# Routing of fourteen of sixteen token tiles moved into the attention stage ahead of it

## The reference

```python
scores = jnp.einsum('bsd,bmd->bsm', hidden_states, memory_tokens) * scale      # second attention
scores = jnp.where(memory_mask[:, None, :], scores, neg_inf)
attn = jax.nn.softmax(scores, axis=-1)
readout = jnp.einsum('bsm,bmd->bsd', attn, memory_tokens)
...
x = hidden_states.reshape(-1, hidden_shape[-1])                                # second mixture of experts
route = jax.nn.sigmoid(x @ router_w)
max_ind = jnp.argmax(route, axis=1)
max_prob = jnp.take_along_axis(route, max_ind[:, None], axis=1)
for e in range(num_experts):
    mask = (max_ind == e)[:, None]
    h = jax.nn.silu(x @ gate_w[e]) * (x @ up_w[e])
    out = out + jnp.where(mask, h @ down_w[e], 0.0)
out = out * max_prob
...
x = x + _L1_xattn_ref(_layernorm(x, axis=-1), ctx_2048, mask_BxS2_bk0)
x = x + _L1_ffn_ref(_layernorm(x, axis=-1), L1_ffn_router_w, L1_ffn_gate_w, L1_ffn_up_w, L1_ffn_down_w)
```

## Time and profile before

| | us |
|---|---|
| runs, median of 3 | 2923.95 (2922.61 to 2924.23) |
| the profiled execution | 2918.47, span 2916.6 |
| second attention, first work to last store issued | 2523.0 to 2715.7 |
| routing, first instruction to last | 2716.7 to 2761.5 |
| expert slots | from 2762.7 to the end |

### The profile page before, as it was taken

How to read it: one execution, slowest core, us unless ns; L and a number is a source line. 1 busy time by engine, 2 the same in 40 slices (tenths; PEclk the granted TensorE clock), 3 DMA queues, 4 the chain that set the end, 5 groups by cost and what they waited for, 6 DMA issues and landing times. The chain is left out here.

```text
span 2916.6 us, 57647 instructions
## 1 busy us (share of the span) xinstructions
PE 2780.5 (95%) x18157; PEld 2443.6 (84%) x18157; DVE 2052.8 (70%) x4824; ACT 1974.1 (68%) x4918; POOL 1697.1 (58%) x2124
## 2 busy tenths in 40 slices
PE   7989999799999999999999999999999997699698
PEld 5768888699999999999999999999999984499655
DVE  7974454577777777777777777777777758866444
ACT  5656666677777777777777777777777747666211
POOL 6766663365665665665666666556656537387122
PEclk9999999899999999999999999999999989899699
DMA  5447767612111111211111111121111014464510
GB/s 181 134 145 213 209 206 206 205 43 71 56 43 61 52 56 43 70 56 43 70 51 48 48 66 56 43 71 56 43 64 49 15 50 91 120 195 131 191 37 27
DMA packets 284601, 263.44 MB, mean 90 GB/s; under 512 B 46382, under 2 KB 260527, under 8 KB 284304
## 3 DMA queue, kind: packets, MB, share of 16 engines
q1 hardware_dynamic: 264784, 238.94, 25.8%
q10 hardware_dynamic: 17312, 15.73, 1.9%
q0 software_dynamic: 2208, 5.12, 0.6%
HBM read 167.34 MB, written 84.93 MB: 86 GB/s over the span
## 5 line engine op out<-in xcount | busy, mean ns | idle before, releaser
L1030 ACT ACTIVATE w_hi<-ps_t 128x512 fp32r<-128x512 f32 (+2 forms) x1024 | 568.4, 555 | 352.3 <-PE ps_t L1273 343.8
L1132 DVE TENSOR_TENSOR w_lo<-ps_t,w_hi 128x512 fp32r<-128x512 f32 (+2 forms) x1024 | 655.7, 640 | 178.8 <-ACT w_hi L1030 175.4
L1106 DVE TENSOR_REDUCE piece_max<-ps_s 128x1 f32<-128x512 f32 (+1 forms) x768 | 472.2, 622 | 238.2 <-PE ps_s L1260 221.6
L1293 PE MATMUL ps_o<-w_hi,v_hi 128*128 128x256 f32 (+1 forms) x1856 | 596.4, 321 | 0.0
L1203 POOL TENSOR_SCALAR prob<-prob,inv_sum 128x512 f32<-128x512 f32 (+2 forms) x768 | 477.8, 641 | 189.2 <-DVE inv_sum L1122 189.2
L1295 PE MATMUL ps_o<-w_hi,v_lo 128*128 128x256 f32 (+1 forms) x1856 | 523.6, 282 | 0.0
L1294 PE MATMUL ps_o<-w_lo,v_hi 128*128 128x256 f32 (+1 forms) x1856 | 522.3, 281 | 0.0
L1273 PE MATMUL ps_t<-ident,prob 128*128 128x128 f32 (+1 forms) x2784 | 517.8, 273 | 0.0
L1273 PEld LDWEIGHTS ps_t<-ident,prob 128*128 128x128 f32 (+1 forms) x2784 | 356.7, 140 | 62.8 <-DVE w_lo L1132 8.7
L1258 PE MATMUL ps_s<-k_hi,q_hi 128*128 128x512 f32 (+2 forms) x1024 | 395.9, 387 | 10.2 <-PEq L57 4.8
L1259 PE MATMUL ps_s<-k_lo,q_hi 128*128 128x512 f32 (+2 forms) x1024 | 377.6, 369 | 0.0
(11 more groups left out here) (288 smaller groups left out, 6352.3 us busy)
## 6 DMA issues: line engine op xcount, KB each, us to landing
v_scratch<-v_out SPq DMA_DIRECT2D x120, 256.0 KB, 3.0
raw_k<-k_scratch SPq DMA_DIRECT2D x32, 960.0 KB, 7.0
raw_v<-v_scratch SPq DMA_DIRECT2D x32, 960.0 KB, 4.7
k_scratch<-k_out SPq DMA_DIRECT2D x104, 256.0 KB, 2.7
q_scratch<-out_t SPq DMA_DIRECT2D x64, 256.0 KB, 2.5
r_all<-r_scratch SPq DMA_DIRECT2D x32, 512.0 KB, 4.2
raw_q<-q_scratch SPq DMA_DIRECT2D x32, 512.0 KB, 5.2
first_prob<-in_ctx_t ACTq DMA_DIRECT2D x50, 256.0 KB, 2.8
```

The source lines that it names most:

```text
L1030: nc.scalar.activation(pt_hi[keys, k % RING, cols], ps_t[keys, k % 2, cols], ACT.Copy).then_inc(hi_done, 1)
L1106: nc.vector.tensor_reduce(piece_max[:, n % 2, p:p + 1], ps_s[:, p, lo - p * PC:hi - p * PC], AX.X, ALU.max).then_inc(max_ready, 1)
L1132: nc.vector.tensor_tensor(pt_lo[keys, k % RING, cols], ps_t[keys, k % 2, cols], pt_hi[keys, k % RING, cols].bitcast(F32), ALU.subtract).th ...
L1293: nc.tensor.matmul(out, v_hi[gi][keys, vs], pt_hi[keys, k % RING, cols], start=blk == (0 if qt else 1), stop=False)
```

## The change

- The router, mean and variance, root, scores, best score and index become tensors that the attention fills for tiles 0 to 13 (`EARLY_ROUTED` is 14). `route_to_slots` does these steps for tiles 14 and 15 alone, and then goes on as before.
- In the attention, tile t is measured by DVE in unit t + 1 behind `add_x` (and behind the penalty where there is one). POOL takes its root at the end of unit t + 1. DVE normalises its rows in step 0 of unit t + 2, behind the inverse sum. PE turns the two halves of the rows in the calls that turn pieces 1 and 2 of unit t + 3, each ahead of the piece, into the 128 free columns of the same bank of ps_t; ACT copies each half ahead of the piece's high part. PE makes the eight logits ahead of piece 0 of unit t + 4, and ACT their exponential. DVE finishes two tiles at a time (`choose`) in step 2 of even units from 6 on. Tiles 12 and 13 go through ps_s in units 14 and 15, when it is free.
- The sigmoid is made of an exponential, plus one, and a reciprocal.
- The router's load moves to the head of the attention, between the mask loads and the first context rows. The three expert weights get a semaphore each, and PE waits for each only where it is first used.

```diff
+EARLY_ROUTED = NT - 2
...
                 for j in range(2):
                     load_mask(j, j)
+                sp.dma_start(router[:, :, :], router_dram.rearrange("(c p) e -> p c e", p=P)).then_inc(router_loaded, 16)
                 for x in range(4):
                     load_r(0, x)
...
+                def root_next(t):
+                    pool.wait_ge(measured, t + 1)
+                    nc.gpsimd.tensor_scalar(var_eps[:, t:t + 1], next_mean_var[:, t, 1:2], LN_EPS, 1.0, ALU.add, ALU.mult).then_inc(eps_added, 1)
+                    pool.wait_ge(eps_added, t + 1)
+                    nc.gpsimd.tensor_tensor(next_rstd[:, t:t + 1], var_eps[:, t:t + 1], half[:, 0:1], ALU.pow).then_inc(rooted, 1)
...
+                        if 0 <= i * UB + u - 1 < EARLY_ROUTED:
+                            root_next(i * UB + u - 1)
...
+                def copy_half(n, c):
+                    t, half_at = n - 3, c - 1
+                    act.wait_ge(next_xt_ready, 2 * t + c)
...
+                    nc.scalar.activation(next_xt[:, t % 2, half_at, :], ps_t[:, (n * SL + c) % 2, AT:AT + P], ACT.Copy).then_inc(next_xt_copied, 1)
...
                     act.wait_ge(pt_ready, i * UB * SL + k + 1)
+                    if c in (1, 2) and 0 <= i * UB + u - 3 < TAIL:
+                        copy_half(i * UB + u, c)
+                    if c == 0 and 0 <= i * UB + u - 4 < TAIL:
+                        score_exponential(i * UB + u)
...
+                def measure(t):
+                    dve.wait_ge(x_added, t + 1)
+                    nc.vector.bn_stats(stats[:, t, :], x_sb[:, t, :]).then_inc(stats_ready, 1)
+                    dve.wait_ge(stats_ready, t + 1)
+                    nc.vector.bn_aggr(next_mean_var[:, t, :], stats[:, t, :]).then_inc(measured, 1)
+
+                def normalise_next(t):
+                    dve.wait_ge(rooted, t + 1)
+                    if t >= 3:
+                        dve.wait_ge(next_xt_ready, 2 * (t - 2))
+                    nc.vector.tensor_scalar(next_xn[:, t % 3, :], x_sb[:, t, :], next_mean_var[:, t, 0:1], next_rstd[:, t:t + 1],
+                                            ALU.subtract, ALU.mult).then_inc(next_xn_ready, 1)
...
                                 if u % 2 == 0 and not last:
                                     penalty(i, u // 2 + 2)
+                                if 0 <= i * UB + u - 1 < EARLY_ROUTED:
+                                    measure(i * UB + u - 1)
+                            if s == 0 and 0 <= i * UB + u - 2 < EARLY_ROUTED:
+                                normalise_next(i * UB + u - 2)
+                            if s == 2 and u % 2 == 0 and i * UB + u >= 6:
+                                choose((i * UB + u - 6) // 2)
...
+                    if c in (1, 2) and 0 <= i * UB + u - 3 < TAIL:
+                        turn_half(i * UB + u - 3, c - 1, ps_t[:, k % 2, AT:AT + P]).then_inc(next_xt_ready, 1)
+                    if c == 0 and 0 <= i * UB + u - 4 < TAIL:
+                        route_next(i * UB + u - 4, ps_t[:, k % 2, AT:AT + E1]).then_inc(logits, 1)
...
-                pe.wait_ge(w_loaded[0], w_loaded[1])
```

More of the change, by code:

```diff
@@ L2084, in add_x, with choose @@
                     nc.vector.scalar_tensor_tensor(x_t, ps_o[:, u % 2, 0:D], inv_sum[:, u % 2:u % 2 + 1], x_t, ALU.mult, ALU.add).then_inc(x_added, 1)
+                def measure(t):
[9 more added lines that the diff above has]
+                                            ALU.subtract, ALU.mult).then_inc(next_xn_ready, 1)
+                def choose(g):
+                    two = slice(2 * g, 2 * g + 2)
+                    dve.wait_ge(score_exps, 2 * g + 2)
+                    nc.vector.tensor_scalar(score_den[:, two, :], score_exp[:, two, :], 1.0, None, ALU.add).then_inc(score_dens, 1)
+                    dve.wait_ge(score_dens, g + 1)
+                    nc.vector.reciprocal(score[:, two, :], score_den[:, two, :]).then_inc(scored, 1)
+                    dve.wait_ge(scored, g + 1)
+                    for t in (2 * g, 2 * g + 1):
+                        nc.vector.max(best[:, t, :], score[:, t, :]).then_inc(maxed, 1)
+                    for t in (2 * g, 2 * g + 1):
+                        dve.wait_ge(maxed, t + 1)
+                        nc.vector.max_index(best_at[:, t, :], best[:, t, :], score[:, t, :]).then_inc(indexed, 1)
                 def scale_rstd(first, end):
@@ L2153, in _ @@
                 add_x(LAST, UB - 1)
+                choose(EARLY_ROUTED // 2 - 1)
+                dve.wait_ge(indexed, EARLY_ROUTED)
             @block.tensor
@@ L2215, in products, with turn_half, route_next, turn_tail @@
                     last.then_inc(pv_done, 1)
+                def turn_half(t, c, out):
+                    pe.wait_ge(next_xn_ready, t + 1)
+                    return nc.tensor.transpose(out, next_xn[:, t % 3, c * P:c * P + P], ident[:, :])
+                def route_next(t, out):
+                    if t == 0:
+                        pe.wait_ge(router_loaded, 16)
+                    pe.wait_ge(next_xt_copied, 2 * t + 2)
+                    for c in range(DC):
+                        last = nc.tensor.matmul(out, next_xt[:, t % 2, c, :], router[:, c, :], start=c == 0, stop=c == DC - 1)
+                    return last
+                def turn_tail(t):
+                    pe.wait_ge(max_ready, NT * SL)
+                    for c in range(DC):
+                        last = turn_half(t, c, ps_s[:, t % 2, c * P:c * P + P])
+                    last.then_inc(next_xt_ready, 2)
                 for v in range(2):
@@ L2232, in body @@
                             products(i, u, s)
+                            if s == 2 and i * UB + u >= TAIL + 2:
+                                turn_tail(i * UB + u - 2)
+                            if s == 3 and i * UB + u >= TAIL + 2:
+                                route_next(i * UB + u - 2, ps_s[:, 2 + u % 2, 0:E1]).then_inc(logits, 1)
                             if s == 2 and exists(u + 3, last):
@@ L2248, with route_to_slots @@
 FACTS = 4
-def route_to_slots(nc, x_sb, router_dram, weights_dram, weights, w_loaded, mean_var, rstd, half, ident, upper_bf, ones_bf, iota,
+def route_to_slots(nc, x_sb, route, weights_dram, weights, w_loaded, half, ident, upper_bf, ones_bf, iota,
                    read_at, write_at, fact, expert_of):
+    router, _, mean_var, rstd, score, best, best_at = route
+    LATE = NT - EARLY_ROUTED
+    late = slice(EARLY_ROUTED, NT)
     with ExitStack() as ctx:
         sb, psum, sem = scope(ctx, nc)
-        norm = norm_memory(sb, sem, "norm4")
-        router = sb("router6", [P, DC, E1])
-        xn = sb("xn6", [P, NT, D])
-        xt = sb("xt6", [P, 2, 2 * DC * P])
-        score = sb("score6", [P, NT, E1])
-        best = sb("best6", [P, NT, 8])
-        best_at = sb("best_at6", [P, NT, 8], U32)
+        stats = sb("stats6", [P, LATE, 6])
+        var_eps = sb("var_eps6", [P, LATE])
+        xn = sb("xn6", [P, LATE, D])
+        xt = sb("xt6", [P, LATE * DC * P])
+        score_exp = sb("score_exp6", [P, LATE, E1])
+        score_den = sb("score_den6", [P, LATE, E1])
         best_f = sb("best_f6", [P, NT])
@@ L2310, in _ @@
             def _(sp):
-                sp.dma_start(router[:, :, :], router_dram.rearrange("(c p) e -> p c e", p=P)).then_inc(router_loaded, 16)
-                for dst, src in zip(weights, weights_dram):
-                    sp.dma_start(dst[:, :, :, :], src.rearrange("e (c p) n -> p e c n", p=P)).then_inc(w_loaded, 16)
+                for dst, src, loaded in zip(weights, weights_dram, w_loaded):
+                    sp.dma_start(dst[:, :, :, :], src.rearrange("e (c p) n -> p e c n", p=P)).then_inc(loaded, 16)
             @block.vector
@@ L2466, in _ @@
                 nc.gpsimd.iota(token[:, :], [[P, NT]], base=1, channel_multiplier=1, allow_small_or_imprecise_dtypes=True).then_inc(tokens_made, 1)
-                for part in range(NORM_PARTS):
-                    norm_rstd(nc, pool, mean_var, rstd, half, norm, part)
+                pool.wait_ge(var_ready, LATE)
+                nc.gpsimd.tensor_scalar(var_eps[:, :], mean_var[:, late, 1], LN_EPS, 1.0, ALU.add, ALU.mult).then_inc(eps_added, 1)
+                pool.wait_ge(eps_added, 1)
+                nc.gpsimd.tensor_tensor(rstd[:, late], var_eps[:, :], half[:, 0:LATE], ALU.pow).then_inc(rooted, 1)
 def moe_slots(nc, x_rows, rows_written, weights, out_rows, ident, read_at, write_at, fact, expert_of, w_loaded):
```

129 lines of the change are left out of this document (81 added, 48 removed).

## The result

| | before | after |
|---|---|---|
| median of the runs, us | 2922.61 (2920.34 to 2924.23, 5 runs) | 2932.45 (2930.83 to 2937.6, 5 runs) |
| profiled execution, span, us | 2918.47, 2916.6 | 2930.83, 2929.0 |

The changed kernel is slower, by 0.3 to 0.4%. The forecast of 2922.0 was wrong, and so was its range, whose end was 2932: it had the change take 2.0 us off, and 9.8 were added.

The account below looks back on a forecast made before the run. PE, busy 142.8 of 143 us, bounds the attention; a chain of short steps bounds the routing. Terms -20.1 + 8.7 + 0.8 + 0.5 + 6.8 + 1.3 = -2.0 gave 2922.0 us; range 2917 to 2927, eight in ten 2913 to 2932.

Parts of the forecast that it names:

- routing's chain: Routing, first DVE operation to copy of best scores: 28.2 us falls to 8.1 with two tiles, so 20.1 us go.
- PE's additions: Attention: transposes and logits of the early tiles, 0.65 us a tile on a PE without idle time, add 8.7 us.
- end of the block: Behind DVE's last update of x: last logits, exponential and small steps for tiles 12 and 13 add 0.8 us.
- start: Head of the attention: the router's 8 KB load ahead of the first context rows adds 0.5 us, between 0 and 1.7.
- DVE held, odd units 3 to 11: POOL's r_lo holds DVE's row normalisation, so PE waits 1.15 us at transpose_x in each of these units.
- DVE held, unit 12: The same r_lo holds DVE's row normalisation in unit 12 and costs about 1.0 us.
- DVE held, even units 2 to 10: Normalisation arrives at 4.8 us, gets in at 5.1 when POOL's t_lo ends, and costs nothing that matters.
- gather beside the last weight: After routing, the first gather goes out while the last expert weight loads, and lands 1.3 us later; bounds 0 and 7.
- The second rival: DVE held in both parities: even units lose 5.8 us more, xt_lo waits 6.6; +10.4 us, 2934.4; chance 0.15.
- The thin cover of xt_lo: Even units: DVE's list ends at 11.0 to 11.4 us, xt_lo is due at 11.8; gone if DVE loses 0.4 more.
- its picture of the loop: Attention growth below 8 or above 25 us would mean the prices of PE's additions or the whole picture are wrong.

Follow-up runs that it names:

- e_no_rows: The changed kernel without DVE's row normalisation in the attention, PE turning rows that are not normalised: 2911.4 us, ratio 0.996 to the kernel before.
- e_rows_first: The changed kernel with the row normalisation between the reciprocal and the last step of the inverse sum: 2928.55 us, ratio 1.0025 to the kernel before.
- e_before_row: The kernel before with only an extra DVE row normalisation per unit at the same place, its output unused: 2940.78 us, ratio 1.0067.
- e_act_rows: The changed kernel with rows normalised by ACT in step 2 ahead of high_x, POOL making the shift: 2913.54 us, ratio 0.9974 to the kernel before.
- e_behind_update: The changed kernel with the row normalisation moved behind the update of x, ahead of penalty and measurement: 2912.81 us, ratio 0.9971 to the kernel before.
- e_act_rows_again: e_act_rows unaltered, measured again beside the changed kernel: 2915.04 us, ratio 0.9969 to the kernel before.
- e_down_later: e_behind_update with `choose` behind the low part of x and the third expert weight loaded after the first two gathers: 2916.98 us, ratio 0.9987.
- e_changed_again: The changed kernel unaltered, measured again: 2931.86 us, ratio 1.0031 to the kernel before.
- e_router_late: The changed kernel with the router's load behind the context rows of the attention's head: 2928.82 us, ratio 1.0026 to the kernel before.
- e_strided: The changed kernel with the normalisation walking its columns with a stride of two: 2927.03 us, ratio 1.0015 to the kernel before.
- e_two_columns: The changed kernel with the normalisation cut to two of 256 columns, PE turning rows not normalised: 2930.27 us, ratio 1.0027 to the kernel before.

## Why the prediction was wrong

Its steps in their order, in us:

| term | forecast | measured |
|---|---|---|
| routing's chain | -20.1 | -20.2 |
| PE's additions | +8.7 | +7.6 (e_no_rows), +7.5 and +9.9 (rows on ACT), waits of 1.2, 0.4 and 2.5 in them |
| end of the block | +0.8 | +0.5 |
| start | +0.5 | 0, within a scatter of 5 |
| DVE held, odd units 3 to 11 | +5.8 | +6.3 idle |
| DVE held, unit 12 | +1.0 | +0.5 idle |
| DVE held, even units 2 to 10 | 0 | +8.4 idle |
| low clock behind the longest stall, rest | 0 | +1.9, what is left of 24.75 |
| gather beside the last weight | +1.3 | +2.6 |
| sum, with +7.6 in the second row | -2.0 | +7.6 |

The step that failed is "In an even unit ... DVE arrives at 4.8 and gets in at 5.1, which costs nothing that matters". POOL was about where the step had it: in unit 6 t_lo ended 0.49 us behind the inverse sum's start; by the prediction's own times (5.1, and 4.35 with the copy's 0.19) it was 0.56. But the step had only the normalisation come to that point. The inverse sum comes first, is an operation of the same kind, waited for t_lo itself and took the place; the normalisation and r_lo then start within 0.02 us of each other, and it was the normalisation that was held. e_rows_first shows this by exchanging the two, e_no_rows and e_before_row that this operation at this place is enough for the stall. It made 8.4 of the 9.6 us by which the sum is off. The step could have been worked out: the earlier trace rows give the inverse sum 0.23 us and the earlier trace rows end t_lo 0.03 us ahead of its end, and the prediction took those 0.23 us as its own length.

The rule drawn on there (the Trainium skill, SBUF — State Buffer, Who interferes with whom) also says that a DVE instruction with two SBUF inputs contends with a GpSimd instruction that reads SBUF. The inverse sum is one, and its 1.81 us in e_rows_first agree. I had applied the rule to tensor_scalar alone. The sentence of the Trainium skill, in the same section, that ACT never waits on anyone agrees with e_act_rows (592 to 602 ns).

The second rival named the outcome (DVE held in both parities, slower), at 2934.4, but not the way: it asked for POOL to reach r_lo before 4.8, and put 6.6 us on waits for xt_lo. POOL was not early; the stall was 1.6 to 2.1 us in an even unit, not 1.15, for the inverse sum's own wait comes on top; and PE never waited for xt_lo, since the penalty was no longer held. That its 2934.4 lies near the measured time is therefore partly luck. The odd units came out near their price (1.18 us in four of them, 1.52 in unit 5, against 1.15), but with a margin of 0.03 us in place of 0.18; by e_rows_first they are held even when the normalisation's record begins ahead of r_lo's. The thin cover of xt_lo showed elsewhere: in e_behind_update (2.9 us), e_act_rows_again (2.0) and e_no_rows (1.0). The attention's 24.75 us lie just inside the 25 at which the prediction would have given up its picture of the loop.

The gather's term had the right cause, shown by e_down_later, and half the size: the stores beside context loads were too mild a row for a gather beside a 4 MB load.

What stays open: the stages sum to +7.6 us, a ratio of 1.0026, and the two measurements gave 1.004 and 1.0031. A ratio of 1.0026 lies inside the interval of the second and just below that of the first, [1.0028, 1.0052]. The rest, 1.5 to 4 us, lies in the profiled pair in the start and in stages that weren't changed. Why the inverse sum passes in odd units, and which part of the last 1.9 us in the attention is the clock's, isn't shown either.

## What to carry to other kernels

Before an operation is put between two others of an engine that shares something with a neighbour, list every operation there that needs the shared thing, tiny ones too, and let each of them wait, in order: here the first took the gap when it was there 0.2 us or more before the neighbour's operation ended, and the next one waited for the neighbour's whole next operation. A duration of 0.4 us says nothing about such an operation; two columns cost as much as 256. Moving that one operation to ACT, or behind the update of x, turned 0.3 to 0.4% slower into 0.3% faster than before.

## What the runs showed of the hardware

- A DVE operation with one output column and two inputs in SBUF (the inverse sum, 0.15 us) was held 1.81 us by POOL, as one of 256 columns was.
- Which record starts first didn't decide who was held: in the odd unit of e_rows_first the normalisation's row starts 0.04 us ahead of r_lo's, in the even unit above 0.02 us ahead, and it is held for all of r_lo in both.
- One wait of 2.13 us in a busy PE was followed by a granted clock of 0.62 over 4.3 us; the waits of 1.2 to 1.6 us weren't followed by a lower one (1.00 from 2592 to 2720). Other traces: 0.60 behind unit 2's wait of 2.13, 2.13, 2.12 and 2.05 us in e_changed_again, e_router_late, e_strided and e_rows_first, 0.63 behind one of 3.21 in e_two_columns, and 1.00 behind one of 2.00 in e_two_columns and of 1.65 in e_before_row.
- A 128 KB gather beside a 4 MB load brought its rows 2.6 us later (7.86 against 5.25 before and 5.26 in e_down_later).
